# Routing a mixture of experts in two parts, with five full blocks computed while the rest is routed

## What is computed

```python
logits = jnp.einsum('bsd,de->bse', input, Wg)          # input: layernorm(h), 1088 x 256; 8 experts
probs = jax.nn.softmax(logits, axis=-1)
top_vals, top_idx = jax.lax.top_k(probs, 2)
top_vals = top_vals / jnp.sum(top_vals, axis=-1, keepdims=True)
...
h = relu(einsum('ebsd,edh->ebsh', xm, W1) + b1)        # 256 -> 512, only for the two experts picked
y = einsum('ebsh,ehd->ebsd', h, W2) + b2               # 512 -> 256
out = jnp.sum(y * scores, axis=0)                      # and h + out is returned
```

## Time and profile before

| | us |
|---|---|
| time, median of 3 runs | 356.38 (355.01 to 358.85) |
| the profiled execution, its time | 357.04 |
| its span | 354.5 |
| PE busy | 330.6 (93% of the span) |
| DVE, ACT, POOL busy | 205.8, 128.3, 140.3 |
| granted TensorE clock, mean | 0.99 |

### The profile page before, as it was taken

How to read it: one execution, slowest core, us unless ns; L and a number is a source line. 1 busy time by engine, 2 the same in 40 slices (tenths; PEclk the granted TensorE clock), 3 DMA queues, 4 the chain that set the end, 5 groups by cost and what they waited for, 6 DMA issues and landing times.

```text
span 354.5 us, 7992 instructions
## 1 busy us (share of the span) xinstructions
PE 330.6 (93%) x2829; PEld 300.3 (85%) x2830; DVE 205.8 (58%) x433; ACT 128.3 (36%) x303; POOL 140.3 (40%) x189
## 2 busy tenths in 40 slices
PE   8889999999999999999979999989999898998983
PEld 7658989999999999999968878845899897997961
DVE  2065398658477867869781148873374454454442
ACT  1168561353625224342332544230323223243211
POOL 5870234241142322142037752123356665565410
PEclk9999999999999999999999999998999999999997
DMA  6971014023030410000000035213777777577166
GB/s 164 311 248 44 2 62 178 2 89 105 2 105 2 172 52 2 2 0 3 3 2 0 2 97 205 87 48 96 239 212 201 230 202 210 171 235 192 49 222 215
DMA packets 19698, 39.55 MB, mean 112 GB/s; under 512 B 2896, under 2 KB 11152, under 8 KB 19536
## 3 DMA queue, kind: packets, MB, share of 16 engines
q1 hardware_dynamic: 17232, 32.54, 29.6%
q0 software_dynamic: 2432, 6.56, 6.5%
HBM read 32.60 MB, written 6.49 MB: 110 GB/s over the span
## 4 chain that ended last, share of the span: by engine, by line
PE 75%; DMA 8%; DVE 8%; issue 4%; SPq 1%; ACT 1%; POOL 1%; DVEq 0%; ACTq 0%; POOLq 0%
PE ps L747 9%; PE ps L879 7%; PE ps L480 7%; PE ps L654 7%; PE ps L670 7%; PE ps L482 6%; PE ps L481 6%; DMA xg<-xrows,gather_u 5%; PE ps L634 3%; PE ps L892 3%; PE ps L635 2%; PE ps L636 2%; PE ps L894 2%; PE ps L494 2%; PE ps L893 2%
## 5 line engine op out<-in xcount | busy, mean ns | idle before, releaser
L480 PE MATMUL ps<-xnhi,wlo 128*128 128x272 f32 x192 | 57.6, 300 | 0.0
L1282 DVE RECIPROCAL invU<-U 128x272 f32<-128x272 f32 x32 | 57.6, 1827 | 0.0
L481 PE MATMUL ps<-xnlo,whi 128*128 128x272 f32 x192 | 55.3, 288 | 0.0
L482 PE MATMUL ps<-xnhi,whi 128*128 128x272 f32 x192 | 55.3, 288 | 0.0
L1160 ACT ACTIVATE hr<-ps,b 128x128 f32<-128x128 f32 x96 | 27.4, 369 | 65.6 <-PE ps L879 65.6
L1640 POOL TENSOR_TENSOR qA<-qraw,invU 128x544 f32<-128x544 f32 x16 | 22.4, 1400 | 71.0 <-DVE invU L1282 36.1
L879 PE MATMUL ps<-xt,w 128*128 128x128 f32 x384 | 47.1, 276 | 1.4 <-DVE xt L1534 1.3
L879 PEld LDWEIGHTS ps<-xt,w 128*128 128x128 f32 x384 | 44.7, 192 | 2.3 <-DVE xt L1534 2.1
L1289 DVE TENSOR_TENSOR pb<-ps,causal 128x592 uint32<-128x592 uint32 (+3 forms) x32 | 27.3, 854 | 28.7 <-PE ps L654 28.5
L747 PE MATMUL ps<-wo,oT 128*128 128x264 f32 x144 | 36.6, 394 | 0.6 <-ACT oT L1043 0.6
L480 PEld LDWEIGHTS ps<-xnhi,wlo 128*128 128x128 f32 x192 | 36.1, 188 | 0.8
(11 more groups left out here) (190 smaller groups left out, 629.5 us busy)
## 6 DMA issues: line engine op xcount, KB each, us to landing
w<-w SPq DMA_DIRECT2D x32, 512.0 KB, 4.7
wraw<-w_attn SPq DMA_DIRECT2D x8, 384.5 KB, 3.3
xrows<-xrow SPq DMA_DIRECT2D x16, 128.0 KB, 1.8
yin<-yrows SPq DMA_DIRECT2D x8, 256.0 KB, 4.1
pt<-patches SPq DMA_DIRECT2D x5, 288.0 KB, 6.1
wv<-w_v SPq DMA_DIRECT2D x4, 256.0 KB, 3.2
oT<-w_ot SPq DMA_DIRECT2D x1, 1024.0 KB, 11.2
wo<-w_o SPq DMA_DIRECT2D x2, 512.0 KB, 11.7
```

What stands on the lines that cost most here:

```text
L480: pe.matmul(dst, slo, mhi[n], start=(i == 0), stop=False)
L481: pe.matmul(dst, shi, mlo[n], start=False, stop=False)
L482: last = pe.matmul(dst, shi, mhi[n], start=False, stop=(i == len(pairs) - 1))
L1282: dve.reciprocal(invU[:, g * GT:(g + 1) * GT], U[:, g * GT:(g + 1) * GT]).then_inc(s_a, 1)
```

## The change

The first FT = 6 tiles hold 1536 rows. Eight experts can leave at most 127 rows each outside of full blocks, so at least NF = 5 blocks are full. Once six tiles are counted, the first five full blocks get their table, their owners and their gathers. The remaining NR = 19 blocks get theirs once all nine tiles are counted. The total stays at 24.

The table is made in another way. `find_ranks` writes `in_slot`, for each row a 1 in the column of its (expert, j-th block of the expert) among 8 x 9 = 72 slots. PE's `slots` multiplies `in_slot` by `at_place` into 72 x 128, ACT copies this out (`keep_slots`), and PE's `tabulate` multiplies it by a small 0/1 matrix (`map1`, `map2`) that says which slot becomes which block. `at_place` of the first four tiles is made by POOL (`mark_places`), of the others by DVE.

Also changed: `xrows` holds each token once (10 DMAs in place of 18). `hrhi` is made by ACT. `turn_x` and `down` use one PSUM bank each in place of two in turn. The useless matmuls and the copy of block counts go. `tell_filled` lags two blocks in place of one, and POOL issues `gather(b + 5)` behind `scatter(b)` in place of ahead of it. `up(23)` is moved ahead of `down(22)`. `weigh` moves from step 2 to step 8.

```diff
...
-            sp.wait_ge(s_owner, 1)
-            for b in range(1, NB):
+                p0, at = DUP if r == RT - 1 else 0, 1 + token0(r)
+                sp.dma_start(xrows[at + p0:at + P], xrow[p0:P, r]).then_inc(s_xrows if r < FT else s_xlate, 16)
+            def load_w1(b):
                 e = sp.value_load(owner_i[0:1, b:b + 1], min_val=0, max_val=E - 1)
-                if b == XG - 1:
-                    sp.wait_ge(s_gx[0], 16)
-                    sp.wait_ge(s_gx[1], 16)
                 if b >= XG:
                     sp.wait_ge(s_up, b - XG + 1)
                 sp.dma_start(w1[b % XG][:], w_1[:, bass.ds(e, 1), :].rearrange("p o n -> p (o n)")
                              ).then_inc(s_w1[b % XG], 16)
+            for r in range(FT):
+                keep_rows(r)
...
+            def slots(r0, r1, by_pool=False):
+                part = r0 // FT
+                if part:
+                    pe.wait_ge(s_tab, 2)
+                for r in range(r0, r1):
+                    pooled = r < 4
+                    pe.wait_ge(s_place_p if pooled else s_place, PICKS * (r + 1 if pooled else r - 3))
+                    for i in range(PICKS):
+                        k = PICKS * r + i
+                        last = pe.matmul(ps[0:SLOTS, 6, (1 + part) * P:(2 + part) * P], in_slot[:, k].rearrange("p e j -> p (e j)"),
+                                         at_place[:, k, :], start=(r in (0, FT) and i == 0), stop=(r in (FT - 1, RT - 1) and i == PICKS - 1))
+                if r1 in (FT, RT):
+                    last.then_inc(s_slots, 1)
+            def tabulate(part):
+                pe.wait_ge(s_kept, part + 1)
+                pe.wait_ge(s_map, part + 1)
+                if part == 0:
+                    last = pe.matmul(ps[:, 6, 0:MW], slot_rows[0][0:SLOTS], map1[0:SLOTS], start=True, stop=True)
+                else:
+                    for i in range(2):
+                        last = pe.matmul(ps[:, 6, 0:NR + NR % 2], slot_rows[i][0:SLOTS], map2[0:SLOTS], start=(i == 0), stop=(i == 1))
...
-            out_part(6, 0, HP)
+            out_part(6, 0, 4)
             count(4)
-            out_part(7, 0, 4)
             count(5)
-            out_part(7, 4, HP)
+            out_part(6, 4, HP)
+            out_part(7, 0, 2)
+            slots(0, FT)
+            out_part(7, 2, 5)
+            tabulate(0)
+            out_part(7, 5, HP)
+            out_part(8, 0, 4)
             count(6)
...
+            out_part(8, 4, 6)
+            pe.wait_ge(s_hrow, 7)
+            turn_x(0, 0)
+            out_part(8, 6, HP)
+            turn_x(1, 1)
             pe.wait_ge(s_owner, 1)
             pe.wait_ge(s_w2lo, E)
-            pe.wait_ge(s_hrow, RT)
-            turn_x(0, 0)
-            turn_x(1, 1)
             up(0, 0)
+            count(8)
             up(1, 1)
             turn_x(2, 0)
-            block_step(1, 1)
+            up(2, 0)
+            slots(FT, RT)
+            turn_x(3, 1)
+            down(0, 0)
+            tabulate(1)
+            pe.wait_ge(s_owner, 2)
             block_step(2, 0)
...
             down(NB - 3, 1)
+            up(NB - 1, 1)
             down(NB - 2, 0)
             pe.wait_ge(s_filled, low_blocks)
...
+                act.wait_ge(s_hr, b + 1)
+                if not early(b, 2):
+                    act.wait_ge(s_dn, b - 1)
+                act.activation(hrhi[par][:], hr[par][:], ACT.Copy).then_inc(s_hrhi, 1)
...
+            def keep_slots(part):
+                act.wait_ge(s_slots, part + 1)
+                act.activation(slot_rows[part][0:SLOTS], ps[0:SLOTS, 6, (1 + part) * P:(2 + part) * P], ACT.Copy
+                               ).then_inc(s_kept, 1)
...
                 link(dve.tensor_scalar(high[:, a], rank_f[:, a], 0.5 - P / 2, P * 1.5 * 2.0 ** 23, ALU.add, ALU.add))
                 link(dve.tensor_scalar(high[:, a], high[:, a], P * 1.5 * 2.0 ** 23, None, ALU.subtract))
...
+                link(dve.tensor_tensor(at_j[:, 0:PICKS * n], high[:, a].unsqueeze(2).to_broadcast([P, PICKS * n, BN]),
+                                       block_start[:, 0:BN].unsqueeze(1).to_broadcast([P, PICKS * n, BN]), ALU.is_equal))
+                dve.tensor_tensor(place_of[:, a], rank_f[:, a], high[:, a], ALU.subtract)
+                dve.tensor_tensor(in_slot[:, a],
+                                  pick[:, r:r + n].bitcast(F32).rearrange("p r i e -> p (r i) e").unsqueeze(3).to_broadcast(
+                                      [P, PICKS * n, E, BN]),
+                                  at_j[:, 0:PICKS * n].unsqueeze(2).to_broadcast([P, PICKS * n, E, BN]), ALU.mult
+                                  ).then_inc(s_placed, n)
...
+            def choose_full():
+                dve.wait_ge(s_count, FT)
+                dve.tensor_tensor(more[:, :, 0:FT], total1, full_steps[:], ALU.is_gt).then_inc(s_full, 1)
+                dve.wait_ge(s_full, 1)
+                link(dve.tensor_reduce(full[:, 1:1 + E], more[:, :, 0:FT], AX_X, ALU.add))
+                link(dve.tensor_tensor_scan(before1[:], ones_e[:], full[:, 0:E], 0.0, ALU.mult, ALU.add))
+                dve.tensor_tensor(chosen[:, 0], before1[:], slot_mask[:], ALU.mult)
+                link(dve.tensor_tensor(chosen[:, 1], full[:, 1:1 + E], slot_mask[:], ALU.mult))
+                link(dve.tensor_reduce(of_slot[:], chosen[:], AX_X, ALU.add))
+                link(dve.tensor_tensor(valid[:], j_of[:], of_slot[:, 1:2], ALU.is_lt))
+                dve.tensor_scalar(map1[:], no_less_j[:, 0:MW], of_slot[:, 0:1], valid[:, 0:1], ALU.is_equal, ALU.mult
+                                  ).then_inc(s_map, 1)
+                link(dve.tensor_tensor(passed[:, 0:NF], before1[:].unsqueeze(1).to_broadcast([P, NF, E]), block_no[:, 0:NF], ALU.is_le))
+                link(dve.tensor_reduce(owner[:, 0:NF], passed[:, 0:NF], AX_X, ALU.add))
+                dve.tensor_scalar(owner_i[:, 0:NF], owner[:, 0:NF], -1.0, None, ALU.add).then_inc(s_owner, 1)
+            def settle_full():
+                link(dve.tensor_scalar(taken[:], before1[:], -1.0, float(NF), ALU.mult, ALU.add))
+                link(dve.scalar_tensor_tensor(taken[:], taken[:], 0.0, full[:, 1:1 + E], ALU.max, ALU.min))
+                link(dve.tensor_tensor(unused[:], j_of[:], of_slot[:, 0:1], ALU.add))
+                link(dve.tensor_scalar(unused[:], unused[:], float(NF), valid[:, 0:1], ALU.is_lt, ALU.mult))
+                link(dve.tensor_scalar(unused[:], unused[:], -1.0, 1.0, ALU.mult, ALU.add))
+            def choose_rest():
+                dve.wait_ge(s_count, RT)
+                link(dve.scalar_tensor_tensor(left[:], taken[:], -float(P), total, ALU.mult, ALU.add))
+                link(dve.tensor_tensor(more[:], left[:].unsqueeze(2).to_broadcast([P, E, BN]), steps[:], ALU.is_gt))
+                link(dve.tensor_reduce(blocks[:, 1:1 + E], more[:], AX_X, ALU.add))
+                link(dve.tensor_tensor_scan(before[:], ones_e[:], blocks[:, 0:E], 0.0, ALU.mult, ALU.add))
+                link(dve.tensor_tensor(left[:], before[:], taken[:], ALU.subtract))
+                link(dve.tensor_tensor(left[:], left[:], slot_mask[:], ALU.mult))
+                link(dve.tensor_reduce(offset[:], left[:], AX_X, ALU.add))
+                dve.tensor_scalar(map2[:], no_less_j[:, 0:NR + NR % 2], offset[:, 0:1], unused[:, 0:1], ALU.is_equal, ALU.mult
+                                  ).then_inc(s_map, 1)
+                link(dve.tensor_tensor(passed[:], before[:].unsqueeze(1).to_broadcast([P, NR, E]), block_no[:], ALU.is_le))
+                link(dve.tensor_reduce(owner[:, NF:NB], passed[:], AX_X, ALU.add))
+                dve.tensor_scalar(owner_i[:, NF:NB], owner[:, NF:NB], -1.0, None, ALU.add).then_inc(s_owner, 1)
+                dve.tensor_scalar(filled_i[:, 0:1], before[:, E - 1:E], float(NF), None, ALU.add)
+                dve.scalar_tensor_tensor(filled_i[:, 1:2], before[:, E - 1:E], float(NF), blocks[:, E:E + 1], ALU.add, ALU.add
+                                         ).then_inc(s_counted, 1)
+            def read_table(part):
+                b, n = slice(NF * part, NB if part else NF), NR if part else NF
+                dve.wait_ge(s_tabmm, part + 1)
+                link(dve.tensor_scalar(spare[:, b], ps[:, 6, 0:n], TOK + 0.5, -float(TOK), ALU.is_gt, ALU.mult))
+                dve.scalar_tensor_tensor(gather_u[:, b], ps[:, 6, 0:n], 1.0, spare[:, b], ALU.max, ALU.add).then_inc(s_tab, 1)
+                link(dve.tensor_copy(table[:, b], ps[:, 6, 0:n]))
+                link(dve.tensor_scalar(spare[:, b], table[:, b], 0.5, 1.0, ALU.is_lt, ALU.mult))
+                link(dve.scalar_tensor_tensor(spare[:, b], spare_no[:, b], 1.0, spare[:, b], ALU.add, ALU.mult))
+                dve.scalar_tensor_tensor(scatter_u[:, b], table[:, b], -1.0, spare[:, b], ALU.add, ALU.add).then_inc(s_tab, 1)
...
+            for r in range(4):
+                tile(r)
+            find_ranks(0, 2)
+            tile(4)
+            find_ranks(2, 2)
+            tile(5)
```

(111 more changed lines are left out.)

228 lines of the change are left out of this document (120 added, 108 removed).

## The result

| | before | after |
|---|---|---|
| time, median (lowest to highest) | 355.69 us (353.25 to 358.85, 4 runs) | 375.74 us (373.96 to 376.96, 4 runs) |
| the profiled execution, its time | 357.04 | 375.84 |
| its span | 354.5 | 373.9 |
| granted TensorE clock, mean | 0.990 | 0.977 |

The change makes the kernel slower: ratio 1.0584, 95% interval 1.0505 to 1.0663. The forecast had the direction and not the size: 364.0, range 352 to 373. Some executions run at a lower granted clock and take over 1.5% longer than the fastest of their kernel; the ratios leave them out, the medians do not.

A forecast was written before the change was run, and what follows sets the result against it. The prediction took the blocks to be bound by PE, with GpSimd's queue close behind. Start -5.1, blocks +13.7 and end -1.0 sum to +7.6 on the profiled 357.04: 364.6, or 364.0 on the median, range 352 to 373.

The forecast's parts named there:

- The path through the scatter: In the blocks, add_b2, scatter, gather, landing, next add_b2 takes 9.14 us per two blocks, against PE's 6.82.
- L: A gather's time from issue to landing in the blocks, taken as 3.6 us, bounds 2.8 and 4.2.
- the third rival: In the blocks, the scatter path is covered if gathers land within 2.3 us: 342 us, chance 0.14.
- The blocks: Block 2 to block 20, nine pairs: 82.3 us against 68.61, so +13.7.
- the fourth rival: In the blocks, the clock falls in repeated waits: 14 us on top, 378 us, chance 0.04.
- The start of the blocks: Routing through add_b2(2): early routing fills the hole, add_b2(2) at 259.0 against 264.14, so -5.1.
- The gathers of blocks 0 to 2 started at 231.6 and are in: Ahead of the blocks: first gathers landed by 237.85, so PE's up(0) starts at 238.8.
- That row is normalised at about 245.5: Start of blocks: SyncE passes tile 8's row, then loads W1 of block 3, landing at about 250.8.
- worth the whole excess of 3.81 over 3.41 if nothing else came up: GpSimd's loop in the blocks: the lag of two frees it of waiting for an older scatter's landing.
- The end: Block 20 onward: up(23) ahead of down(22) fills PE's waits, taken as -1, bounds -2.1 and +0.9.
- edits at nothing: Small edits priced at zero, among them halved xrows writes, hrhi on ACT and single banks for turn_x and down.
- the empty front: The start gives nothing, as something beside VectorE's chain costs the 5.1 again: 369 us, chance 0.08.

The follow-up runs named there:

- Experiment 5: Kernel of experiment 2, with SyncE loading W1 of blocks 3 and 4 ahead of keeping tile 8's rows: 354.75 us, ratio 0.9943.
- experiment 6: Kernel of experiment 5, with W1 of blocks 1 and 2 each held until a gather has landed: 351.01 us, ratio 0.9875.
- Experiment 7: Kernel after the change, scatter still first, with only tell_filled lagging by one block again: 377.25 us, ratio 1.0559.
- experiment 4: Kernel before the change, with only tell_filled lagging two blocks in place of one: 361.12 us, ratio 1.0147.
- experiment 9: Kernel of experiment 4, with GpSimd clearing 640 unused columns (some 0.6 us) after each scatter: 353.88 us, ratio 0.9968.
- experiment 11: Kernel of experiment 10, with down writing two PSUM banks in turn: 349.49 us, ratio 0.9811.
- experiment 10: Kernel of experiment 6, with the old order at the end (down(22), loads' signal, up(23)): 352.43 us, ratio 0.9888.
- experiment 1: Kernel after the change, with GpSimd issuing the gather of block b+5 ahead of the scatter of block b again: 361.71 us, ratio 1.0127.
- experiment 2: Kernel after the change, with gather first and tell_filled lagging one block, GpSimd's whole loop as before: 356.93 us, ratio 1.0007.
- experiment 12: Kernel of experiment 11, with tell_filled lagging two blocks and GpSimd clearing 648 finished columns after each scatter: 345.00 us, ratio 0.9729.

## Why the prediction was right or wrong

**The path through the scatter: right.** 5.54 + L for a pair, with L = 3.6, gave 9.14. After 286.70 the pairs measure 9.2 to 9.3 (`add_b2` at 286.70, 296.03, 305.36, 314.57, 323.91 and 333.21), with a gather of 3.43 to 3.64 in them, as forecast (3.6); the last two are 9.77 and 8.97. The other terms measure 5.71 for 5.54 in the round shown (1.23, 1.36 and 3.12 from landing to `add_b2`). In the kernel before with only the order swapped a pair is 9.35. One step on this path was wrong without harm to the sum: "in nearly every step, and in both interleaved chains". The gather ends last in one chain only, after block 5 in 10 of 18 transposes, and PE's wait there is 0.2 to 1.4 us, not 1 or more in each step. The Trainium skill's formula (DMA: Bandwidth & Descriptors, "Anatomy of one DMA — SWDGE (gpsimd) path"), an estimate of 2.3 for a gather, is not met by any of them; the third rival, which needed such gathers, fell. Its threshold of 2.3 does not follow from the rest of the sum: with the 2.84 that the sum uses, 5.54 + L reaches PE's 6.82 at L = 1.3, and at L = 2.3 the pair would be 7.84. No row is named for the 1.8 in its place.

**The blocks: 86.8 for 82.3.** Of the excess of 4.5, 3.3 lie in the first two pairs, 10.18 and 11.38 (265.14, 275.32, 286.70). There the granted clock fell, as the windows of the kernel after show, and in one `down` of each pair the matmuls stand 0.21 apart in place of 0.12:

```profile
265.00:275.00 10.00, 8.02 (x55) 7.60 (x54) 3.37 (x8) 3.55 (x10) 4.45 (x6) 0.83 0.52 161
275.00:287.00 12.00, 9.92 (x73) 9.50 (x72) 3.39 (x7) 5.43 (x14) 4.41 (x6) 0.86 0.50 140
287.00:296.00 9.00, 6.90 (x55) 6.18 (x55) 4.34 (x16) 3.21 (x11) 4.75 (x6) 1.00 0.54 167
```

Twelve such matmuls cost 1.1 us more, so the two `down` make about 2.2, an estimate from these rows. This is a piece of the fourth rival: at most 3.3 us of its 14, not in every wait. That the lower clock makes all 3.3 was not tried; the landings in these pairs (3.58 and 4.31) are slow too.

**The start of the blocks: wrong, the largest miss in the method.** The forecast had `add_b2(2)` 5.1 earlier, and it came 1.0 later, 2.1 of which arose ahead of the routing. The steps that failed are two. The first is "The gathers of blocks 0 to 2 started at 231.6 and are in". They started at 233.5, on time less the 2.1, but landed only at 240.3 and 242.1, the second 7.09 after its issue, because SyncE now issues three W1 loads of 512 KB between 232.1 and 235.1. Before, block 0's W1 was loaded ahead of the routing, and block 2's waited for the first two gathers. The two waits stand as removed lines in the diff, and I priced them at nothing, without saying so. The second is "That row is normalised at about 245.5", "so W1 lands" "at about 250.8". With the gathers late, `up(0)` and ACT's relu were late, the row came at 250.4, and W1 landed at 255.5. Behind each of the two waits (2.92 and 2.81 us of PE) the clock fell too, and `up(0)` and `up(3)` took 3.13 and 3.45 in place of 2.0; the sum had no term for that.

Experiment 5 undoes the second step, experiment 6 the first. From the first `tile` to `add_b2(2)` it is 53.4 us in the kernel after, 50.1 in experiment 5 and 47.9 in experiment 6 (54.5 before). By the times they are worth 2.2 and 3.7 us. With both, `add_b2(0)` is where the forecast had it. That `add_b2(2)` is at 259.19 for 259.0 is partly luck: this execution was 1.6 late, and its gathers go first, so its path isn't the forecast's. VectorE's order, most of the working, was right. GpSimd's places were not: 0.79 each in the first four, where the prediction had 0.3 to 0.6 with no row behind it. The places ended at 230.1 and cost PE a wait of 0.50.

**The lag of `tell_filled`: right in the sum, wrong as a reading of the kernel before.** Experiment 7 shows that it is worth nothing in the kernel after, as the sum took it. But "worth the whole excess of 3.81 over 3.41 if nothing else came up" has the wrong sign where nothing else changes: experiment 4 is 1.5% slower. The wait for a landed scatter also spaced the indirect DMAs out (four take 4.48 us at the least in the blocks of the kernel before). When they are apart by other means (experiment 9), the blocks gain 3.6 of the excess of 7.2.

**The end: -1 forecast, +0.2 measured.** `down(23)` starts 7.64 behind `add_b2(20)` (7.92 before), a gain of 0.3 in place of 2.1, and the first load of `yin` starts 6.13 behind it (3.56 before). "One bank for `turn_x` and one for `down`" stood among the edits at nothing, since inside the loop the reader is done in time. At the end, where `down(21)`, `down(22)` and `down(23)` follow each other without a block between them, it is not, and the single bank puts `add_b2` between them: in the kernel after `down(21)` waits 0.82 us for it and `down(23)` 0.74. With the old order and two banks (experiment 11) the end is 21.7, against 23.9 with one (experiment 10).

**The range** ended at 373: it held the slow gathers (369 by L = 4.2) and the empty front (369) one by one, not together with the clock. Of the 11.8 us of span between forecast and measured (19.4 less 7.6), 6.1 lie in front of `add_b2(2)` (4.0 of them in the front), 4.5 in the blocks and 1.2 at the end. The sum with the measured terms, -1.1 + 2.1 + 18.2 + 0.2, is 19.4.

**Not settled.** The spacing is not the whole rule of the late news. In experiments 1 and 4 there are eight such stretches, each behind four indirect DMAs issued in 4.05 to 4.38 us, and none elsewhere in their blocks. But kernels with a lag of one have them too: three in experiment 2 (its profiled execution took 365.05), one each in experiments 5, 6, 10 and 11, of 2.0 to 4.2 us of ACT's idle time. Only two of these seven stand behind such a group (4.27 and 4.41 us). And in experiment 6 one such group, in 4.28, passed without a stretch. So with the gathers first the lag of two has more of them, and neither kernel with the added work has one. What holds the increments back no trace here shows.

## What to carry to other kernels

An in-order queue that issues both the write of one step and the read of a later one sets the order in which two chains couple: put first what does not depend on the newest result, and here it is 5% of the kernel. When you move a transfer's issue, also list every transfer that the old order kept out of its way, and each wait in the removed lines of the diff: here two small waits on SyncE were worth 3.7 us, where the kernel of experiment 6, early routing and all, is 4.4 us faster than before. A wait that looks useless in the chain can be a spacer; before it is taken out, look at what it keeps apart.

## What was not expected of the hardware

- After four indirect DMAs issued 1.3 to 1.6 us apart TensorE's semaphore increments came up to 3 us late, in 8 of 8 cases in experiments 1 and 4 (idle time of ACT put down to "remote", 3.93 to 5.19 us each). Seven more in five kernels with a lag of one, five of them without such a group. With some 0.65 us of work in each round (experiments 9 and 12) none occurred.
- A gather of 128 rows landed in 7.09 us with three loads of 512 KB issued in the 2.9 us ahead of it. With one such load (experiment 6) the first gather, issued at 233.04, was transposed from 236.79 on. In the later blocks, from 285 us on, the gathers of the chain took 3.4 to 4.0.
- The granted clock fell to 0.83 and 0.86 over stretches of 10 and 12 us in which PE was busy 0.80 and 0.83 of the time, and stayed at 1.00 in the next at 0.77, with the same rhythm.
